# A spectral mixing kernel: folding of the next slab spread over one iteration more, and row 0 transformed at the end of the mixing

## The reference

```python
xf = jnp.fft.rfft2(x, axes=(1, 2), norm='ortho')        # 128 x 65 modes
o1r = relu(xr @ w1[0] - xi @ w1[1] + b1[0])             # per block of 96
o1i = relu(xi @ w1[0] + xr @ w1[1] + b1[1])
o2r = softshrink(o1r @ w2[0] - o1i @ w2[1] + b2[0], 0.01)
o2i = softshrink(o1i @ w2[0] + o1r @ w2[1] + b2[1], 0.01)
out = jnp.fft.irfft2(o2r + 1j * o2i, s=(128, 128), norm='ortho') + x
```

## Time and profile before

| | |
|---|---|
| median of 3 runs | 5081.34 us |
| profiled execution | 5084.92 us, span 5082.8 us |
| PE matmul busy | 4944.4 us (97%) |
| DVE busy | 4024.7 us (79%) |
| ACT busy | 2574.7 us (51%) |
| POOL busy | 1347.3 us (27%) |
| granted TensorE clock | 0.998 |
| chain that ended last | PE 81%, DVE 7%, issue 5%, POOL 3%, ACT 2% |

### The profile page before, as it was taken

One profiled execution on the slowest core, in us unless ns is written; L12 is line 12 of the kernel. 1 busy time (PEld: TensorE's weight loads), 2 busy tenths in 40 slices (PEclk: granted clock), 3 DMA queues, 4 the chain that ended last, 5 costly groups with the idle time before them and its releaser, 6 DMA issues.

```text
span 5082.8 us, 113588 instructions
## 1 busy us (share of the span) xinstructions
PE 4944.4 (97%) x43936; PEld 4268.3 (84%) x43936; DVE 4024.7 (79%) x5484; ACT 2574.7 (51%) x3939; POOL 1347.3 (27%) x1285
## 2 busy tenths in 40 slices
PE   7999999999999999999999999999999999999998
PEld 6888888888888888888888888888888888888887
DVE  6878788787787877878778878788787787877876
ACT  4554555545455554555545554555545455454553
POOL 0331123321233312333123331123321233212333
PEclk9999999999999999999999999999999999999999
DMA  3321333312333123331233322333222333123311
GB/s 109 101 72 52 88 101 101 93 45 74 101 101 105 40 66 101 101 105 50 64 94 101 105 60 63 84 101 105 79 58 70 101 105 92 50 66 101 105 51 50
DMA packets 1067734, 420.99 MB, mean 83 GB/s; under 512 B 1064864, under 2 KB 1064992, under 8 KB 1067168
## 3 DMA queue, kind: packets, MB, share of 16 engines
q1 hardware_dynamic: 1062432, 411.63, 29.9%
q10 hardware_dynamic: 4736, 1.60, 0.1%
HBM read 210.26 MB, written 201.33 MB: 81 GB/s over the span
## 4 chain that ended last, share of the span: by engine, by line
PE 81%; DVE 7%; issue 5%; POOL 3%; ACT 2%; DMA 1%; SPq 1%; DVEq 0%; POOLq 0%; ACTq 0%
PE ps L624 13%; PE ps L528 13%; PE ps L549 9%; PE ps L515 7%; PE ps L633 6%; PE ps L561 5%; PE ps L607 4%; PE ps L595 4%; PE ps L653 3%; PE ps L655 2%; PE ps L654 2%; PE ps L574 2%; PE ps L582 2%; PE ps L575 2%; DVE ring L884 2%
## 5 line engine op out<-in xcount | busy, mean ns | idle before, releaser
L1046 POOL TENSOR_TENSOR turn<-turn 1x1 f32<-1x1 f32 x224 | 46.5, 207 | 3499.3 <-PE ps L528 3499.3
L624 PE MATMUL ps<-wts,hbig 128*128 128x192 f32 x4160 | 731.9, 327 | 4.2
L947 DVE TENSOR_TENSOR biased<-ps,wts 128x768 f32<-128x768 f32 (+1 forms) x544 | 501.0, 921 | 266.6 <-PE ps L633 239.8
L515 PE MATMUL ps<-tab,ring 128*64 128x128 f32 x6144 | 692.7, 274 | 9.8 <-ACT ring L735 3.9
L528 PE MATMUL ps<-tab,ring 128*128 128x128 f32 x6144 | 694.6, 276 | 4.2
L528 PEld LDWEIGHTS ps<-tab,ring 128*128 128x128 f32 x6144 | 688.5, 192 | 10.3 <-DVE ring L1013 10.3
L516 PE MATMUL ps<-tab,ring 128*63 128x128 f32 x6144 | 694.3, 274 | 0.0
L515 PEld LDWEIGHTS ps<-tab,ring 128*64 128x64 f32 x6144 | 670.5, 137 | 26.9 <-ACT ydg L745 8.8
L624 PEld LDWEIGHTS ps<-wts,hbig 128*128 128x128 f32 x4160 | 673.0, 190 | 16.4 <-ACT hbig L806 13.7
L516 PEld LDWEIGHTS ps<-tab,ring 128*63 128x63 f32 x6144 | 670.3, 136 | 0.0
L549 PEld LDWEIGHTS ps<-tab,ydg 128*128 128x128 f32 x4032 | 501.3, 191 | 114.1 <-issue 82.9
(11 more groups left out here) (95 smaller groups left out, 9470.8 us busy)
## 6 DMA issues: line engine op xcount, KB each, us to landing
out<-x SPq DMA_DIRECT2D x352, 480.0 KB, 3.6
x<-in_x SPq DMA_DIRECT2D x192, 768.0 KB, 7.3
x<-in_x SPq DMA_DIRECT2D x32, 816.0 KB, 7.6
x<-in_x SPq DMA_DIRECT2D x32, 720.0 KB, 6.6
out<-x SPq DMA_DIRECT2D x32, 432.0 KB, 4.1
wts<-in_mix SPq DMA_DIRECT2D x16, 513.0 KB, 3.6
out<-x SPq DMA_DIRECT2D x32, 240.0 KB, 3.4
out<-x SPq DMA_DIRECT2D x32, 192.0 KB, 3.6
```

What stands on the lines that cost most here:

```text
L515: pe.matmul(o[0:HALF], slot[:, 0:HALF], mat("fwd_w"), start=True, stop=True)
L624: mm = pe.matmul(o, hbig[:, k * H:(k + 1) * H], mix_part("w2_big"), start=first, stop=False, skip_group_check=True)
L947: dve.tensor_tensor(parts(v), d, b2, ALU.add).then_inc(bias_done, 1)
```

## The change

The folding table becomes (2,1,1,1,1,1): iteration 1 folds chunks 0 and 1, and each of iterations 2 to 6 one more. PE's product for row 0 of slab q + 1 moves from the head of that slab's lines to the end of slab q's mixing, in place of one of the five warming products, and writes bank 2; group 2 of the inverse lines, which uses that bank, waits for ACT's copy. The line groups keep their banks. ACT copies row 0 ahead of its early packs of groups 2 to 4, and issues the two DMAs behind the five packs of the next slab, once PE is through with the rows (`v_done`, `u_done`) and POOL with the first four row groups. At p = 1 that is ahead of the loop's jump. In the last slab, where nothing is folded, a memset sets `pairs_folded`.

```diff
-FOLD_IN = {1: (0, 1, 2), 2: (3,), 3: (4,), 4: (5,), 5: (6,)}
+FOLD_IN = {1: (0, 1), 2: (2,), 3: (3,), 4: (4,), 5: (5,), 6: (6,)}
...
-        ROW0_BANK = 4
+        ROW0_BANK = 2
+        FIRST_BANK = 5
...
-            return (g + ROW0_BANK + 1) % 8 if stage == 0 else g % 8
+            return (g + FIRST_BANK) % 8 if stage == 0 else g % 8
...
                 def forward_lines(q, p):
                     pe.wait_ge(uv_ready, NF * q + NF - 3)
                     wait_batch(pe, q - 1, PLAIN - 1)
-                    pe.wait_ge(pairs_folded, FOLDS * (q + 1))
-                    pe.matmul(ps[:, ROW0_BANK, 0:CB], mat("fwd_w"), xs[p][:, 0, :],
-                              start=True, stop=True).then_inc(row0_done, 1)
                     for g in range(NG):
                         bank = line_bank(0, g)
-                        if g == 7:
-                            pe.wait_ge(row0_copied, q + 1)
-                        elif g > 7:
+                        if g > 7:
                             wait_moved(pe, q, g - 8)
-                        elif g % 2:
+                        elif g % 2 and g < 7:
...
+                def transform_row0(q, p):
+                    pe.wait_ge(pairs_folded, FOLDS * (q + 1))
+                    pe.matmul(ps[:, ROW0_BANK, 0:CB], mat("fwd_w"), xs[p][:, 0, :],
+                              start=True, stop=True).then_inc(row0_done, 1)
+
                 def inverse_lines(q):
                     for g in range(NG):
+                        if g == ROW0_BANK:
+                            pe.wait_ge(row0_copied, q + 2)
...
                 pe.wait_ge(cleared, 1)
+                transform_row0(0, 0)
                 with pe.Fori(0, STEPS) as t:
...
-                        keep_warm(q, 5)
+                        keep_warm(q, 4)
+                        transform_row0(q + 1, 1 - p)
                         inverse_lines(q)
...
-                def move_row0(q):
+                def copy_row0(q):
                     act.wait_ge(row0_done, q + 1)
                     act.copy(row0[:], ps[:, ROW0_BANK, 0:CB]).then_inc(row0_copied, 1)
+
+                def move_row0(q):
                     act.wait_ge(row0_copied, q + 1)
...
                         q = t * PAIRS + p
-                        move_row0(q)
                         lines(q, p)
...
                                  ps[:, E_BANK, 0:2 * CB]).then_inc(merged, 1)
+                        act.wait_ge(row0_moved, 32 * (q + 1))
+                        copy_row0(q + 1)
                         for g in range(2, RING):
                             early_pack(q, g)
...
                             for g in range(RING):
                                 pack_lines(q + 1, 1 - p, g)
+                            act.wait_ge(v_done, NF * q + NF)
+                            act.wait_ge(u_done, NF * q + NF)
+                            wait_batch(act, q, PLAIN - 1)
+                            move_row0(q + 1)
...
                 for g in range(RING):
                     pack_lines(0, 0, g)
+                copy_row0(0)
+                move_row0(0)
...
                         if fold_next:
                             fold_in(q, t, p, 1)
+                        else:
+                            dve.memset(clamped[0:1, 0:1], 0.0).then_inc(pairs_folded, FOLDS)
```

## The result

The changed kernel is slower: 5101.27 us against 5083.08 us, both medians of 7 runs, ratio 1.0034 (95% interval 1.0023 to 1.0045). The forecast was 5069.5, and its range ended at 5086. The profiled execution has a span of 5099.1 us, 16.3 more than before. Where they lie shows best by phase. The table is worked out from the timelines of both kernels: a phase lasts from its first product on PE to the first one of the next, and row 0's product is counted to the phase ahead of it. The jump of ACT's and DVE's loops stands behind an odd slab, so the lines of the even slabs 2 to 28 are the 14 "at a jump".

A forecast was written before the change was run, and what follows sets the result against it. TensorE (PE), busy 4944.4 of 5082.8 us, was taken as the bound. Terms -11.7 (fold), -4.6 and -0.4 (row 0), 0 (inverse lines) and +4.9 (jumps) gave -11.8: median 5081.34 to 5069.5 us, range 5058 to 5086.

The forecast's parts named there:

- (a): Start of a mixing iteration: one fold less before DVE's second remainder ends PE's wait for it, -11.7 us.
- (b): Head of the lines: row 0's product leaves the slab boundary, 0.29 us inside the loop, 0.39 across the jump, 10.5 us.
- (c): Start of the inverse lines: ACT's row 0 copy delays its early packs, DVE's idle time absorbs it, 0 us.
- (d): Head of the lines: ACT jumps only after the rows' end and transfers; first move late, net +0.35 us at 14 jumps.
- I take 3.2: ACT's loop jump: assumed refetch time in us, between ACT's own 2.4 and DVE's 3.95 (bound 4.0).
- The argument for the middle: ACT's loop jump: 3.2 us refetch, since the engine matches ACT's 2.4 us row and the traffic DVE's 3.95 us row.
- The 0.75 us that I let the phase absorb: End of the lines at a jump: part of ACT's lateness returns where PE waits for DVE's last move, between 0 and 1.1.
- The rival with the refetch at DVE's value: ACT's jump: refetch of 3.95 us takes the gain back, +1.1 us a jump, 5080 us; chance 0.27.
- The rival that is not absorbed: ACT's jump: 3.95 us refetch, none of the lateness returning, +2.1 us a jump, 5094 us; chance 0.10.

The follow-up runs named there:

- the fourth experiment: Changed kernel with ACT's waits for the end of the rows still ahead of its loop's jump but the two transfers behind it: 5081.51 us, ratio 0.9997.
- the sixth: Changed kernel with the transfers behind ACT's jump and four waited-for copies of row 0 onto itself between waits and jump: 5138.44 us, ratio 1.0105.
- the second experiment: Changed kernel with the old folding table, so only the move of row 0: 5113.93 us, ratio 1.0058.

## Why the prediction was wrong

The mechanism was the right one, and its price was too low by so much that the sign turned.

(a) *The fold*: -11.7 forecast, -12.2 measured in the mixing, and -12 by the ratio of the fold alone (-10.8 by its medians). Right, and at the place that was named: the weight loads' wait for the remainder.

(b) *Row 0's product*: 10.5 us forecast, 9.0 measured. Inside the loop it was worth 0.2 us a boundary and not 0.29, across the jump 0.39. The 0.29 was the distance from L499's start to the first line's; from the start of the rows' last product it was 0.51 to that line before,

```profile
2390.81 0.38 PE L655 MATMUL ps<-ylo,even_hi 128*128 128x480 f32 x1
```

and is 0.32 now (2398.86 to 2399.18 above), because the line starts later behind that product than L499 did. At its new place it cost nothing: the wait ahead of the inverse lines is 0.32 us a slab as before.

(c) *ACT at the start of the inverse lines*: 0 forecast; 686.7 us before and after. DVE's waits for ACT there did grow, from 91.4 to 111.2 us, and none of it reached PE:

```profile
DVE ylo L907 <- ACT yhi L759: 91.4, 128, 1.4
...
DVE ylo L921 <- ACT yhi L764: 111.2, 128, 2.0
```

(d) *ACT behind the jump*: this is the step that failed. Forecast: ACT's first move 3.4 us after PE's first line; measured 4.6 to 4.9. Of the difference 1.05 us is the refetch: "I take 3.2", between the bounds 2.4 and 4.0, and it took 4.1 to 4.3 us in all 14 cases, above the upper bound. The argument for the middle, that the engine was that of the quiet row and the traffic that of the busy one, was wrong in giving the engine a weight: the same engine's refetch takes 2.5 us in quiet and 4.2 in traffic, and 1.5 of the difference pass before its packet starts. The other 0.3 us are the second transfer, 0.81 us instead of 0.64, and 0.1 to 0.2 us from the end of the rows to the first transfer.

The 0.75 us that I let the phase absorb were right in size: by the same steps, 4.75 + 5.1 - 7.0 = 2.85 us late, less 0.39 and 0.75, is +1.7 a jump, and what was measured is 2.1 in the lines less 0.39. In the timelines group 8 starts 9.7 to 9.9 us after the first line where the clock hasn't fallen (7.04 before), and the phase is 2.1 us longer, so 0.7 come back. But they don't come back where the prediction took them from: PE's wait for DVE's last move is 19.2 us after 19.1. PE lost 0.3 us ahead of group 16 and 0.3 ahead of group 19 in these phases before, and loses nothing there now that it arrives later; the two make up 0.6 of the 0.7.

The rival with the refetch at DVE's value named this case and priced it 1.1 a jump, since it started from 4.2 us between line and move and not from 4.8. The rival that is not absorbed came nearest in time, with 5094 us and +2.1 a jump, but by luck: it started from the same short refetch and priced no clock, and leaving out the 0.7 us that did come back made up for both.

(e) *The clock*, missing from the sum: PE stands still for 2 us, and in five of 14 cases TensorE then runs at 0.50 of its clock. 7 us. A standstill in the middle of a phase had been priced at its own length.

So -12.2 - 9.0 in the parts that were forecast at -22.2, against 14 x 2.1 + 5 x 1.4 = 36 us in the lines at jumps that were forecast at 14 x 0.74 = 10. Of these 26 us too little, 19 are the late first move and 7 the clock.

The rule of the Trainium skill ("Runtime: NRT & Kernel Launch", section "Instruction fetch mechanics"), that a taken branch outside the loaded window fetches its page before going on, agrees with the traces: 2.5 us in quiet, 3.5 and 4.2 us in the stores' traffic, and nothing in the experiment in which ACT has no branch.

## What to carry to other kernels

A loop's jump is free only as long as its engine's queue can run ahead to it: before a wait is put at the end of a loop's body, look at what hides the jump now, and put the waiting work behind the jump and behind the first instructions that others need. Price a refetch by the traffic of the moment at which it will happen, and set the upper bound above the longest value that any engine shows in traffic: the bound of 4.0 us was one row of DVE's, whose jumps took 3.1 to 4.1 us in the kernel before, and ACT's then took 4.1 to 4.3. When PE is the bound, a standstill of 2 us can cost another 1.4 us through the clock, so count it with a margin.

## What the runs showed of the hardware

- ACT's refetch takes 2.4 to 2.7 us when the DMA engines are idle and 4.1 to 4.3 us between the stores, nearly the same in all 14 cases of one kernel; 1.4 us earlier among the same stores it is 3.4 to 3.6 us. The mean DMA share doesn't order these values (0.90, 0.72 and 0.99 for 4.2, 4.3 and 3.5 us).
- The difference lies mostly in the wait for its one packet of 8192 bytes to start: 0.9 to 1.2 us after the branch in quiet, 1.8 to 2.0 in the fourth experiment, 2.45 to 2.5 in the changed kernel and the sixth. The packet itself is no longer in traffic (0.31 to 0.39 us) than in quiet (0.31 to 0.57). Behind which packets it waits was not found out.
- With a first gap of 1.9 to 2.1 us in PE's weight loads, TensorE's granted clock fell to 0.50 in five of 14 phases of the changed kernel and in seven of 14 of the second experiment; with 1.0 to 1.4 us in none; with 3.1 to 3.4 us (the sixth) in all 14; with the gap filled by products in none. Where it fell in the changed kernel, the phase was 1.4 us longer.
- DVE's pack of the same 128 x 508 elements takes 0.68 to 0.83 us or 1.42 to 1.56 us at nearly the same place of the phase, with POOL busy in both. What decides was not tried.
